# Reading the memory inside the first self-attention's loop, and one normalisation for two before the second cross-attention

## The chip, the cores and the metric

One Trainium2 chip, one core of it. A core has TensorE (PE, matrix products into PSUM), VectorE (DVE), ScalarE (ACT), GpSimd (POOL) and SyncE (SP, which starts the transfers), each with a queue of its own that it works off in order; they wait for one another by semaphores. The metric is the time of one execution on the device in microseconds, all in float32.

## The reference, cut to what matters

Two layers of a network run over 64 samples of 32 latent tokens with 128 features (2048 tokens), each with a context of 257 rows. Six blocks add to `x`, each after a normalisation:

```python
x = x + _L0_xattn_ref(_layernorm(x, axis=-1), ctx_1024, ctx_1024, ...)
x = x + _L0_attn_ref(_layernorm(x, axis=-1), L0_attn_Wq, ..., L0_attn_memory, L0_attn_memory_norm, L0_attn_memory_weight)
x = x + _L0_ffn_ref(_layernorm(x, axis=-1), ...)
x = x + _L1_xattn_ref(ctx_1024, _layernorm(x, axis=-1), ...)
x = x + _L1_attn_ref(...)
x = x + _L1_ffn_ref(...)
```

The first self-attention mixes ordinary attention with a memory that is read by the queries:

```python
a_dot = jnp.einsum('bnst,btnd->bsnd', probs, v4)
sigma_q = jax.nn.elu(q.reshape(B, S, N_QUERY, KV))
num = sigma_q @ memory
den = (sigma_q @ memory_norm)[..., None]
a_mem = (num / den).reshape(B, S, QH, D_HEAD)
w = jax.nn.sigmoid(memory_weight)
out = (a_dot * (1.0 - w) + a_mem * w).reshape(B, S, D_MODEL)
```

The second cross-attention gets `_layernorm(x)` and normalises it again, with a gain and an offset:

```python
ln = layer_norm(latents, g_latent, b_latent)   # (t - mu) * rsqrt(var + EPS) * gamma + beta
```

## The kernel before

The program is a chain of stages. Each stage is one or more blocks; a block gives every engine a piece of program, and at its end all engines meet before the next begins. Tensors stand with features on the 128 partitions and tokens along the free axis; `chunk(t, c)` is 512 of the 2048 tokens, so there are `NCH = 4` chunks. `core.bank` is PSUM, eight banks of 512 floats.

`layernorm` is a block of its own: for each chunk TensorE makes the mean (line 185), VectorE subtracts it (195), ScalarE squares (210), TensorE makes the variance (188), ScalarE takes logarithm and exponential for the reciprocal root (213, 215), and VectorE multiplies (199) and, if asked, applies gain and offset (202). Four chunks run staggered. It is called once before each block and twice before the second cross-attention, as `ln3` from `xT` to `yT` and as `ln4` from `yT` to `yT` with gain and offset.

`memory_attention_0` has three blocks. The first projects queries and keys into `qT` and `kT`. The second is the loop: 16 steps of four samples (128 tokens), two steps to one turn of a hardware loop (`Fori`), with n = 2 i + j the step. In a step GpSimd spreads keys and queries over the heads (650, 651), TensorE makes the scores of step n (675), VectorE takes the maximum and subtracts it (783, 785), ScalarE takes the exponential (740); VectorE sums, inverts and normalises the step before (792, 794, 796); TensorE transposes the probabilities of step n - 2 (666), ScalarE copies them as `pT` (727), TensorE multiplies them with the values (686), ScalarE masks the heads apart (735) and VectorE adds them up into `aT`, of step n - 3 (801); TensorE makes the values of step n (695) from tokens that ScalarE copied (754), and ScalarE copies the values (746). The order is written by hand: TensorE does transposes, scores, output product, values; ScalarE tokens, `pT`, exponential, mask, values; VectorE normalises, then maximum and subtraction, then the output. `S` uses banks 0 and 1, `TP`, `OP`, `VP` banks 2 to 4; banks 5 to 7 are unused in the loop.

The third block is the tail, which reads the memory for all 2048 tokens: VectorE takes the minimum with zero (837), ScalarE relu and exponential (859, 861), VectorE puts them together as the activated query `high` (841) and adds the attention's part to `xT` with its gate (843); TensorE makes the numerator (872) and the denominator for two groups of heads (874), ScalarE copies the numerator (864), VectorE inverts the denominators (845), TensorE turns them (877), ScalarE copies that (866), TensorE spreads them over the features (883), VectorE multiplies (850) and adds with the gate (854).

## Time and profile before

| | us |
|---|---|
| median of 3 runs | 1338.82 (1338.72 to 1343.13) |
| the profiled execution | 1347.86 |
| its span | 1346.1 |
| PE, DVE, ACT, POOL busy in it | 1183.1, 796.2, 731.1, 353.0 |

The profile is of one execution, whose span lies 1.8 us below its own time; a sum over its rows is made against 1347.86, and a difference is carried over to the median. Busy time counts what an engine works, waits are the gaps.
### The profile page before, as it was taken

The numbers are of one execution on the slowest core, as the hardware profiler recorded it, in microseconds if no ns is written. First come the engines' busy times: TensorE is split into PE (matmuls) and PEld (weight loads), VectorE is DVE, ScalarE is ACT, GpSimd is POOL, SyncE is SP. The second block draws the span as 40 slices with busy tenths as digits, with TensorE's granted clock in tenths as the row PEclk, the third lists the DMA queues.
The fourth block names the chain that finished last, engine by engine and source line by source line (L and its number), as shares of the span: only waits on it lengthen the run. The fifth ranks groups of instructions, "written<-read, shape, count | busy, mean of one in ns | idle before, by whom it ended". The sixth has DMA issues, their size and how long they took to land. (4 is left out here: it accounts for less than half of the span.)

```text
span 1346.1 us, 39879 instructions
## 1 busy us (share of the span) xinstructions
PE 1183.1 (88%) x14797; PEld 894.6 (66%) x14800; DVE 796.2 (59%) x2937; ACT 731.1 (54%) x1593; POOL 353.0 (26%) x734
## 2 busy tenths in 40 slices
PE   5899999966767699999987799999999999988865
PEld 2677777726655477777773688888888888732333
DVE  2677777756863356565655565555555555447267
ACT  2677777735862145444434455555555555354557
POOL 1121212126600011111110244334443344311132
PEclk8899999988986599999997899999999999998889
DMA  2433333100000333323220454445544455200001
GB/s 58 116 101 76 71 76 72 48 1 1 0 0 5 111 106 95 90 83 92 83 59 8 113 144 124 122 126 133 128 125 122 125 128 133 75 18 0 0 1 32
DMA packets 89480, 101.02 MB, mean 75 GB/s; under 512 B 13128, under 2 KB 78608, under 8 KB 89232
## 3 DMA queue, kind: packets, MB, share of 16 engines
q1 hardware_dynamic: 89360, 99.40, 28.3%
q8 instruction: 77, 1.26, 0.4%
q14 instruction: 43, 0.35, 0.1%
HBM read 87.62 MB, written 11.74 MB: 74 GB/s over the span
## 5 line engine op out<-in xcount | busy, mean ns | idle before, releaser
L1382 POOL TENSOR_TENSOR d_p<-d_p,d_rtotal 128x289 f32<-128x289 f32 x256 | 170.3, 665 | 246.5 <-DVE d_rtotal L1522 246.5
L1516 DVE CUSTOM_DVE_ANT_0 d_p<-bank,d_low 128x289 f32<-128x289 f32 x256 | 112.3, 439 | 180.6 <-PE bank L1411 180.6
L1481 ACT ACTIVATE d_p<-d_p,d_nmax 128x289 f32<-128x289 f32 x256 | 137.7, 538 | 98.7 <-DVE d_nmax L1516 98.6
L1424 PE MATMUL bank<-d_pT,d_xr 32*128 32x128 f32 x5120 | 160.9, 275 | 0.0
L1411 PE MATMUL bank<-x_keyT,d_q 128*128 128x289 f32 x512 | 154.8, 423 | 2.5 <-DVE d_nmax L1516 1.3
L1424 PEld LDWEIGHTS bank<-d_pT,d_xr 32*128 32x128 f32 x5120 | 148.7, 187 | 8.8 <-issue 1.5
L435 ACT ACTIVATE a_p<-a_p,a_nmax 128x257 f32<-128x257 f32 x256 | 109.4, 499 | 75.6 <-DVE a_nmax L468 75.6
L1146 PEld LDWEIGHTS bank<-c_w,c_hs 128*128 128x128 f32 x1024 | 120.9, 194 | 14.8 <-issue 14.8
L1530 DVE STREAM_TRANSPOSE d_pT<-d_p 128x320 f32<-128x320 f32 x256 | 128.4, 502 | 1.1 <-POOL d_p L1382 1.1
L1137 PE MATMUL bank<-yT,c_w 128*128 128x512 f32 x256 | 117.7, 604 | 4.7 <-DMA c_w<-in_L_ffn_w 4.7
L1146 PE MATMUL bank<-c_w,c_hs 128*128 128x128 f32 x1024 | 121.1, 277 | 0.0
L468 DVE CUSTOM_DVE_ANT_0 a_p<-bank,a_low 128x257 f32<-128x257 f32 x256 | 93.8, 423 | 41.8 <-PE bank L385 39.8
L1213 ACT ACTIVATE c_hs<-bank,c_w 128x512 f32<-128x512 f32 x128 | 87.5, 684 | 38.5 <-PE bank L1137 35.5
L1411 PEld LDWEIGHTS bank<-x_keyT,d_q 128*128 128x128 f32 x512 | 81.9, 189 | 33.3 <-DVE d_nmax L1516 18.0
L1205 ACT ACTIVATE x_keyT<-bank 128x512 f32<-128x512 f32 (+2 forms) x33 | 34.7, 1051 | 115.2 <-PE bank L1159 112.1
L1277 DVE SCALAR_TENSOR_TENSOR c_acc<-bank,c_gates,c_acc 128x128 f32<-128x128 f32 x128 | 36.0, 344 | 98.9 <-PE bank L1146 98.9
L1489 ACT ACTIVATE d_a<-bank 128x512 f32<-128x512 f32 x64 | 38.2, 597 | 85.2 <-PE bank L1424 85.2
L1137 PEld LDWEIGHTS bank<-yT,c_w 128*128 128x128 f32 x256 | 47.2, 194 | 52.9 <-issue 47.7
L1401 PEld LDWEIGHTS bank<-yT,x_wqk 128*128 128x128 f32 x512 | 67.7, 194 | 9.9 <-ACT d_q L1474 3.6
L1436 PEld LDWEIGHTS bank<-d_a,x_wvo 128*128 128x128 f32 x512 | 65.4, 191 | 13.1 <-issue 7.3
L1401 PE MATMUL bank<-yT,x_wqk 128*128 128x128 f32 x512 | 68.7, 278 | 2.4 <-ACT d_q L1474 2.4
L1436 PE MATMUL bank<-d_a,x_wvo 128*128 128x128 f32 x512 | 68.2, 277 | 2.0 <-ACT d_a L1489 0.7
(289 smaller groups left out, 2094.4 us busy)
## 6 DMA issues: line engine op xcount, KB each, us to landing
d_xr<-key_rows SPq DMA_DIRECT2D x256, 160.0 KB, 3.1
d_low<-mask_low SPq DMA_DIRECT2D x64, 144.5 KB, 3.4
a_ctT<-in_ctxT SPq DMA_DIRECT2D x64, 128.5 KB, 2.1
a_low<-mask_low SPq DMA_DIRECT2D x64, 128.5 KB, 3.0
c_ct<-in_ctx SPq DMA_DIRECT2D x64, 128.0 KB, 2.3
key_rows<-c_ct SPq DMA_DIRECT2D x128, 64.0 KB, 2.0
c_w<-in_L_ffn_w SPq DMA_DIRECT2D x8, 514.0 KB, 3.8
xT<-in_xT SPq DMA_DIRECT2D x4, 256.0 KB, 3.6
```

The lines of the kernel that those rows point to most:

```text
L435: nc.scalar.activation(P[:, r % 2, g, :], P[:, r % 2, g, :], ACT.Exp, bias=nmax[:, r % 2, g:g + 1], scale=-1.0).then_inc(exp_made, 1)
L468: nc.vector.tensor_tensor_reduce(P[:, r % 2, g, :], S[g], low[:, r % RING, :], -1.0, 3.4e38, ALU.add, ALU.min, accum_out=nmax[:, r % 2, g: ...
L1137: nc.tensor.matmul(UP[k], w[:, j, 128 * k:128 * k + 128], chunk(core.yT, c), start=True, stop=True).then_inc(up_made, 1)
L1146: ins = nc.tensor.matmul(Y[s % 2][:, m, :], hs[:, s % 2, k, 128 * m:128 * m + 128], w[:, j, HID + 128 * k:HID + 128 * k + 128], start=(k = ...
L1382: nc.gpsimd.tensor_tensor(p, p, rtotal[:, b % 2, g:g + 1].broadcast_to([128, KEYS]), ALU.mult).then_inc(normed, 1)
L1401: ins = nc.tensor.matmul(Q[:, 128 * h:128 * h + 128], wqk[:, 4 * r + h, :], latT[:, bass.ds((i * 2 + ahead) * 128, 128)], start=True, stop ...
L1411: nc.tensor.matmul(S[u % 2], q[:, b // 4, b % 4, 4 * g:4 * g + 4, :].rearrange("p h q -> p (h q)"), keyT[:, bass.ds(i * EIGHT + b, 1), :]. ...
L1424: ins = nc.tensor.matmul(O[j], xr[rows, b % 2, k, :], pT[rows, b % 2, :, 32 * k:32 * k + 32], start=(k == 0), stop=(k == BLOCKS - 1))
L1436: ins = nc.tensor.matmul(OUT, wvo[:, h, :], a[:, ago % 2, h].rearrange("p b q -> p (b q)"), start=(h == 0), stop=(h == HEADS - 1))
L1481: nc.scalar.activation(p, p, ACT.Exp, bias=nmax[:, b % 2, g:g + 1], scale=-1.0, accum_out=total[:, b % 2, g:g + 1]).then_inc(exp_made, 1)
L1516: nc.vector.tensor_tensor_reduce(P[:, b % 2, g, 0:KEYS], S[u % 2], low[:, b % 4, :], -1.0, 3.4e38, ALU.add, ALU.min, accum_out=nmax[:, b % ...
L1530: nc.vector.transpose(pT[:, b % 2, g, :], P[:, b % 2, g, :]).then_inc(turned, 1)
```

## The change

The third block of `memory_attention_0` is gone. Its work is done by a function `retrieve(n)` in the queue of each of the three engines, once in every step of the loop, behind the step's own work. `due(n, delay)` tells whether a part is due: a chunk c has its parts in the steps 3 c + delay. Minimum, relu and exponential have delay 0, putting together 1, numerator and denominator 2, the inverse, its turning and the copy of the numerator 3, the copy of the turned inverse 4, the spreading 5, product and gated addition 6. The attention's own gated addition of a chunk (`attended`) follows when its four steps of output are done, in the steps 7, 11 and 15, and once behind the loop. The parts use banks 5 to 7, one chunk at a time, so further waits guard each bank and the small tiles. The loops are no longer hardware loops but written out, on all four engines.

The two normalisations before the second cross-attention become one from `xT` to `yT` with gain and offset; the variance goes into the logarithm as var (1 + EPS) + EPS squared, which is what the two roots come to one behind the other. A constant tile for it is set at the start of the program.

```diff
--- before.py
+++ after.py
...
-def layernorm(core, name, src, dst, gamma=None, beta=None):
+def layernorm(core, name, src, dst, gamma=None, beta=None, twice=False):
...
-                    nc.scalar.activation(chunk(rstd, s - 1), var[:, s - 1, :], ACT.Ln, bias=core.eps[:, 0:1]).then_inc(log_ready, 1)
+                    nc.scalar.activation(chunk(rstd, s - 1), var[:, s - 1, :], ACT.Ln, bias=(core.eps_twice if twice else core.eps)[:, 0:1],
+                                         scale=1.0 + EPS if twice else 1.0).then_inc(log_ready, 1)
...
+            NUM, SPREAD = core.bank[:, 5, :], core.bank[:, 7, :]
+            DEN, TURNED = core.bank[:, 6, 0:8], core.bank[0:8, 6, 128:256]
...
+            STEP = 3
             block = loop.enter_context(nc.Block())
+
+            def due(n, delay):
+
+                c, rest = divmod(n - delay, STEP)
+                return c if rest == 0 and 0 <= c < NCH else None
...
-                peeled(pool, GROUPS // 2, body)
+                unrolled(GROUPS // 2, body)
...
+                    retrieve(n)
+
+                def retrieve(n):
+
+                    c = due(n, 2)
+                    if c is not None:
+                        pe.wait_ge(elu_made, c + 1)
+                        if c:
+                            pe.wait_ge(num_kept, c)
+                            pe.wait_ge(turned_kept, c)
+                        nc.tensor.matmul(NUM, mem[:], chunk(high, c), start=True, stop=True)
+                        for m in range(4):
+                            ins = nc.tensor.matmul(DEN[:, 2 * m:2 * m + 2], high[:, 512 * c + 128 * m:512 * c + 128 * m + 128], norm[:], start=True, stop=True)
+                        ins.then_inc(num_made, 1)
+                    c = due(n, 3)
+                    if c is not None:
+                        pe.wait_ge(inverted, c + 1)
+                        nc.tensor.transpose(TURNED, inverse[:], core.ident[:]).then_inc(turned, 1)
+                    c = due(n, 5)
+                    if c is not None:
+                        pe.wait_ge(turned_kept, c + 1)
+                        if c:
+                            pe.wait_ge(weighed, c)
+                        for m in range(4):
+                            ins = nc.tensor.matmul(SPREAD[:, 128 * m:128 * m + 128], place[0:8, m].rearrange("r s d -> r (s d)"), inverse_t[:], start=True, stop=True)
+                        ins.then_inc(spread, 1)
...
-                with pe.Fori(2, GROUPS // 2) as i:
+                for i in range(2, GROUPS // 2):
...
+                def retrieve(n):
+
+                    c = due(n, 0)
+                    if c is not None:
+                        nc.scalar.activation(chunk(high, c), chunk(qT, c), ACT.Relu).then_inc(relu_made, 1)
+                        act.wait_ge(clipped, c + 1)
+                        nc.scalar.activation(chunk(low, c), chunk(low, c), ACT.Exp).then_inc(expd, 1)
+                    c = due(n, 3)
+                    if c is not None:
+                        act.wait_ge(num_made, c + 1)
+                        act.wait_ge(elu_made, c + 1)
+                        nc.scalar.activation(chunk(low, c), NUM, ACT.Copy).then_inc(num_kept, 1)
+                    c = due(n, 4)
+                    if c is not None:
+                        act.wait_ge(turned, c + 1)
+                        if c:
+                            act.wait_ge(spread, c)
+                        nc.scalar.activation(inverse_t[:], TURNED, ACT.Copy).then_inc(turned_kept, 1)
...
                     values(0, j)
+                    retrieve(j)
...
+                def retrieve(n):
+
+                    c = due(n, 0)
+                    if c is not None:
+                        nc.vector.tensor_scalar(chunk(low, c), chunk(qT, c), 0.0, None, ALU.min).then_inc(clipped, 1)
+                    c = due(n, 1)
+                    if c is not None:
+                        dve.wait_ge(relu_made, c + 1)
+                        dve.wait_ge(expd, c + 1)
+                        nc.vector.scalar_tensor_tensor(chunk(high, c), chunk(low, c), -1.0, chunk(high, c), ALU.add, ALU.add).then_inc(elu_made, 1)
+                    c = due(n, 3)
+                    if c is not None:
+                        dve.wait_ge(num_made, c + 1)
+                        if c:
+                            dve.wait_ge(turned, c)
+                        nc.vector.reciprocal(inverse[:], DEN).then_inc(inverted, 1)
+                    c = due(n, 6)
+                    if c is not None:
+                        dve.wait_ge(num_kept, c + 1)
+                        dve.wait_ge(spread, c + 1)
+                        nc.vector.tensor_tensor(chunk(low, c), chunk(low, c), SPREAD, ALU.mult).then_inc(weighed, 1)
+                        dve.wait_ge(weighed, c + 1)
+                        nc.vector.scalar_tensor_tensor(chunk(core.xT, c), chunk(low, c), gate[:, 2:3], chunk(core.xT, c), ALU.mult, ALU.add).then_inc(chain, 1)
+
+                def attended(c):
+
+                    dve.wait_ge(o_copied, 4 * c + 4)
+                    dve.wait_ge(chain, c + 1)
+                    nc.vector.scalar_tensor_tensor(chunk(core.xT, c), chunk(aT, c), gate[:, 3:4], chunk(core.xT, c), ALU.mult, ALU.add)
...
+                        retrieve(i * 2 + j)
+                        if (i * 2 + j) % 4 == 3 and i * 2 + j >= 7:
+                            attended((i * 2 + j - 7) // 4)
...
+                attended(NCH - 1)
...
-    layernorm(core, "ln3", core.xT, core.yT)
...
-        layernorm(core, "ln4", core.yT, core.yT, affine[:, 2:3], affine[:, 3:4])
+        layernorm(core, "ln3", core.xT, core.yT, affine[:, 2:3], affine[:, 3:4], twice=True)
```

TensorE in the loop, before: one step from the values of a step on (695 values, 666 transposes, 675 scores, 686 output product), inside the hardware loop.

```order
L695 MATMUL bank<-wb_wv,b_yg 128x128 x4
L666 MATMUL bank<-ident,b_p 128x128 x4
L671 REGISTER_ALU
L675 MATMUL bank<-b_kb,b_qb 128x128 x4
L686 MATMUL bank<-b_pT,b_vb 128x128 x4
L695 MATMUL bank<-wb_wv,b_yg 128x128 x4
```

And after, from the values of step 5 to those of step 6 (709 values, 721 numerator, 723 denominator, 735 spreading, 680 transposes, 689 scores, 700 output product).

```order
L709 MATMUL bank<-wb_wv,b_yg 128x128 x4
L721 MATMUL bank<-b_high,wb_mem 128x512
L723 MATMUL bank<-b_norm,b_high 128x2 x4
L735 MATMUL bank<-b_inverse_t,b_place 128x128 x4
L680 MATMUL bank<-ident,b_p 128x128 x4
L689 MATMUL bank<-b_kb,b_qb 128x128 x4
L700 MATMUL bank<-b_pT,b_vb 128x128 x4
L709 MATMUL bank<-wb_wv,b_yg 128x128 x4
```

Numerator, denominator and spreading now stand between a step's values and the transposes and scores of the next.

ScalarE in the loop, before (746 values, 754 tokens, 727 `pT`, 740 exponential, 735 mask), from the values of step 2 on, the same order as in the hardware loop:

```order
L746 ACTIVATE b_vb<-bank 32x4x32 x4
L754 ACTIVATE b_yg<-yT 128x512
L727 ACTIVATE b_pT<-bank 128x512
L740 ACTIVATE b_p<-b_p 128x512
L735 ACTIVATE b_odiag<-bank,b_own_head 128x4x32 x4
L746 ACTIVATE b_vb<-bank 32x4x32 x4
```

And after, from the values of step 3 on (786 values, 800 relu, 802 exponential, 807 numerator, 794 tokens, 767 `pT`, 780 exponential of step 4).

```order
L786 ACTIVATE b_vb<-bank 32x4x32 x4
L800 ACTIVATE b_high<-b_qT 128x512
L802 ACTIVATE b_low<-b_low 128x512
L807 ACTIVATE b_low<-bank 128x512
L794 ACTIVATE b_yg<-yT 128x512
L767 ACTIVATE b_pT<-bank 128x512
L780 ACTIVATE b_p<-b_p 128x512
```

Three operations now stand between the values and the tokens of the next step, in every third step.

VectorE after, in step 6 (863 output, 870 minimum, 881 inverse, 886 product, 888 gated addition, 854 to 858 the normalising of that step):

```order
L863 TENSOR_REDUCE b_aT<-b_odiag 128x128
L870 TENSOR_SCALAR b_low<-b_qT 128x512
L881 RECIPROCAL b_inverse<-bank 128x8
L886 TENSOR_TENSOR b_low<-b_low,bank 128x512
L888 SCALAR_TENSOR_TENSOR xT<-b_low,wb_gate,xT 128x512
L854 TENSOR_REDUCE b_total<-b_p 128x16
L856 RECIPROCAL b_rtotal<-b_total 128x16
L858 TENSOR_TENSOR b_p<-b_p,b_rtotal 128x512
```

Before, the output was followed straight by the sum of line 792; four operations now stand between.

## Rows read from the trace of the kernel before

**Rows 1.** Stage table: start:end, length; busy (instructions) per engine; PEclk granted clock; DMA share; GB/s.
```profile
302.00:323.00 21.00, 11.91 (x68) 11.26 (x69) 12.07 (x15) 8.16 (x22) 14.99 (x41) 0.76 0.00 1
323.00:380.00 57.00, 41.24 (x342) 38.77 (x341) 47.00 (x73) 47.67 (x135) 31.91 (x88) 1.00 0.00 0
391.50:418.00 26.50, 21.40 (x73) 16.62 (x74) 12.87 (x21) 6.91 (x14) 0.00 (x0) 0.50 0.00 1
```

**Rows 2.** Timeline, one loop step: start, length, engine, line, operation, [idle before <-releaser].
```profile
361.05 0.63 ACT L754 ACTIVATE b_yg<-yT 128x512 f32 x1
...
361.70 0.60 ACT L727 ACTIVATE b_pT<-bank 128x512 f32<-128x512 f32 x1
361.79 0.69 DVE L785 TENSOR_TENSOR b_p<-bank,b_top 128x512 f32<-128x512 f32 x1
...
362.35 1.16 PE L686 MATMUL bank<-b_pT,b_vb 128*128 128x128 f32 x8 [1.32 <-ACT b_pT L727]
...
362.52 0.63 ACT L740 ACTIVATE b_p<-b_p 128x512 f32<-128x512 f32 x1 [0.22 <-DVE b_p L785]
...
363.35 1.06 PE L695 MATMUL bank<-wb_wv,b_yg 128*128 128x128 f32 x8
...
363.63 1.14 ACT L735 ACTIVATE b_odiag<-bank,b_own_head 128x128 f32<-128x128 f32 x4 [0.48 <-PE bank L686]
...
364.24 0.60 PE L666 MATMUL bank<-ident,b_p 128*128 128x128 f32 x4
...
364.64 1.09 ACT L746 ACTIVATE b_vb<-bank 32x128 f32<-32x128 f32 x4
364.68 1.06 PE L675 MATMUL bank<-b_kb,b_qb 128*128 128x128 f32 x8
365.75 0.63 ACT L754 ACTIVATE b_yg<-yT 128x512 f32 x1
365.77 0.69 DVE L783 TENSOR_REDUCE b_top<-bank 128x16 f32<-128x512 f32 x1 [0.69 <-PE bank L675]
```

**Rows 3.** Timeline: first and last operation of the tail, and the next normalisation.
```profile
391.80 0.63 ACT L859 ACTIVATE b_high<-b_qT 128x512 f32<-128x512 f32 x1 [1.37 <-PEq L623]
...
416.95 0.75 DVE L854 SCALAR_TENSOR_TENSOR xT<-b_qT,wb_gate,xT 128x512 f32<-128x512 f32 x1
417.97 1.28 ACT L206 ACT_TABLE_LOAD   x1 [9.09 <-PEq L823]
```

**Rows 4.** Timeline: TensorE in the tail.
```profile
400.76 2.06 PE L872 MATMUL bank<-b_high,wb_mem 128*128 128x512 f32 x2
...
402.61 1.71 PE L874 MATMUL bank<-b_norm,b_high 128*128 128x2 f32 x8
...
408.93 7.19 PE L883 MATMUL bank<-b_inverse_t,b_place 32*128 32x128 f32 x32 [0.35 <-ACT b_inverse_t L866]
```

**Rows 5.** Timeline, start of the loop; last, line 796 (times ns: min/median/max).
```profile
310.37 3.82 DVE L796 TENSOR_TENSOR b_p<-b_p,b_rtotal 128x512 f32<-128x512 f32 x1
...
313.25 0.40 POOL L651 TENSOR_TENSOR b_qb<-b_qT,b_own_head 128x128 f32<-128x128 f32 x1
...
317.22 0.77 DVE L796 TENSOR_TENSOR b_p<-b_p,b_rtotal 128x512 f32<-128x512 f32 x1
...
317.91 0.68 DVE L783 TENSOR_REDUCE b_top<-bank 128x16 f32<-128x512 f32 x1
...
323.70 0.69 DVE L783 TENSOR_REDUCE b_top<-bank 128x16 f32<-128x512 f32 x1 [1.99 <-PE bank L675]
...
L796 DVE TENSOR_TENSOR b_p<-b_p,b_rtotal x16: 691/692/3821, 310.4 to 383.2; 128x512 f32<-128x512 f32 x16
```

**Rows 6.** Timeline: first operations of the two normalisations and of the stage behind.
```profile
718.99 1.28 ACT L206 ACT_TABLE_LOAD   x1 [7.54 <-PEq L1043]
...
732.38 1.28 ACT L206 ACT_TABLE_LOAD   x1 [1.01 <-PEq L165]
...
746.49 3.27 PEld L1454 LDWEIGHTS bank<-ident,yT 128*128 128x128 f32 x16 [3.79 <-issue]
```

More of the change, by code:

```diff
@@ L35, in __init__ @@
         self.rows_moved = self.sem("rows_moved")
-        self.eps = self.sb("eps", [128, 1])
+        self.eps, self.eps_twice = self.sb("eps", [128, 1]), self.sb("eps_twice", [128, 1])
         self.spent, self.spent_sems = ExitStack(), []
@@ L155, in _ @@
             nc.gpsimd.memset(core.eps[:], EPS).then_inc(built, 1)
+            nc.gpsimd.memset(core.eps_twice[:], EPS * EPS).then_inc(built, 1)
             pool.wait_ge(built, 1)
@@ L637, in memory_attention_0 @@
             t_made, t_copied, o_made, o_masked, o_copied = (sem(f"b_{n}") for n in ("t_made", "t_copied", "o_made", "o_masked", "o_copied"))
+            low, high = sb("b_low", [128, TOK]), sb("b_high", [128, TOK])
+            inverse, inverse_t = sb("b_inverse", [128, 8]), sb("b_inverse_t", [8, 128])
+            NUM, SPREAD = core.bank[:, 5, :], core.bank[:, 7, :]
+            DEN, TURNED = core.bank[:, 6, 0:8], core.bank[0:8, 6, 128:256]
+            clipped, relu_made, expd, elu_made, num_made, num_kept, inverted, turned, turned_kept, spread, weighed, chain = (
+                sem(f"b_{n}") for n in ("clipped", "relu_made", "expd", "elu_made", "num_made", "num_kept", "inverted", "turned", "turned_kept", "spread", "weighed", "chain"))
+            STEP = 3
             block = loop.enter_context(nc.Block())
+            def due(n, delay):
+                c, rest = divmod(n - delay, STEP)
+                return c if rest == 0 and 0 <= c < NCH else None
             @block.gpsimd
@@ L766, in _ @@
                     values(1, j)
-                with act.Fori(2, GROUPS // 2) as i:
+                    retrieve(2 + j)
+                for i in range(2, GROUPS // 2):
                     for j in range(2):
@@ L810, in body @@
                             output(i, j - 3)
+                        retrieve(i * 2 + j)
+                        if (i * 2 + j) % 4 == 3 and i * 2 + j >= 7:
+                            attended((i * 2 + j - 7) // 4)
                 body(0, 0)
                 body(1, 1)
-                with dve.Fori(2, GROUPS // 2) as i:
+                for i in range(2, GROUPS // 2):
                     body(i, 2)
```

58 lines of the change are left out of this document (removed).

## The prediction

> **What bounds the kernel now.** I read the stage table first, then one step of the self-attention loop in the timeline, then the tail behind the loop, then the three normalisations. The whole program is a chain of stages, each ended by a block boundary that all engines pass, so the last engine of each stage counts, and shares of the whole span say little. The change touches two stretches: the first self-attention (loop and tail), and the two normalisations before the second cross-attention.
>
> The loop does 16 steps of 128 tokens. In its steady part, 323 to 380 us [rows 1], no engine is full (VectorE 47.0, ScalarE 47.7, TensorE 41.2 of 57 us), so a ring of waits bounds it. One step [rows 2] shows it: ScalarE copies pT (361.70); 0.65 later TensorE starts the output product (362.35); 1.28 later ScalarE masks it (363.63); 1.01 later it copies the values (364.64), 1.11 later the tokens (365.75), and as after the copy of tokens at 361.05, 0.65 later the next pT. Sum 0.65 + 1.28 + 1.01 + 1.11 + 0.65 = 4.70, just the distance of the two token copies (365.75 - 361.05). ScalarE rests only 0.70 in it (0.22 ahead of the exponential, 0.48 ahead of the mask), VectorE 0.69 (ahead of the maximum), TensorE 1.32 (ahead of the output product); the brackets behind the rows say so. Those three gaps are all the cover there is.
>
> The tail reads the memory: 391.80 to the start of the next normalisation at 417.97 [rows 3], 26.2 us. TensorE works in it at a granted clock of 0.50, 1.2 of 2.4 GHz [rows 1], and its products are most of it: four times 2.06 for the numerator plus 1.71 for the denominator, then 7.19 to spread [rows 4].
>
> **The change part by part.** *The tail goes*: -26.2 us. What comes back is the four gated additions of the attention; three lie in the loop, the last stays behind it with its 0.75 (the same form as the multiply-add at 416.95) [rows 3]. Before, the boundary behind the last addition took 0.27 (417.97 - 416.95 - 0.75) and there was one from loop to tail of the same kind; one of the two goes with the tail.
>
> *The same work in the loop.* Per chunk of 512 tokens, every third step, prices at the full clock, which the loop has [rows 1]: TensorE gets numerator, denominator and spread. Their rows, halved, allow up to 2.06 / 2 = 1.03, 1.71 / 2 = 0.86 and 7.19 / 4 / 2 = 0.90; each holds the drain of its last product, which the next one covers, so I take 0.86 for each. ScalarE gets relu and exponential (0.63 each [rows 3]) and the copy of the numerator (0.60, as pT [rows 2]), less the overlap of neighbours, 0.63 against 0.55 from row to row, so 1.63; and a copy of 8x128, about one of the four in row 364.64, 0.2 to 0.3. VectorE gets five operations, none longer than the 0.75 of row 416.95 and the reciprocal of eight columns far shorter, and on average one gated addition of 0.75: 3 to 3.5 in all.
>
> Where they stand decides, and there are three kinds of step (n is the step, remainder by three):
> 1. Remainder 1: the small copy goes into ScalarE's ring, 4.70 + 0.2 = 4.9. VectorE's subtraction of one (0.7) takes its gap of 0.69.
> 2. Remainder 2: numerator, denominator and (from n = 5) spread stand behind the value product, and in front of the transposes that the next pT needs. From pT: 0.65 to the output product, 1.00 to the values (362.35 to 363.35) [rows 2], 0.89 for these (363.35 to 364.24 is their pitch, by eight instructions of 0.11), then 3 x 0.86, and transposes and semaphore 0.65. Sum 5.77, so +1.1.
> 3. Remainder 0: TensorE is now late, so the ring starts at its transposes: 0.44 to the scores, 1.09 to the maximum (364.24, 364.68, 365.77) [rows 2], 0.72 to the subtraction (361.79, a step earlier), 0.73 to the exponential (362.52), 0.55 to the mask, 1.01 and 1.11 as before, then relu, exponential and numerator copy 1.63, and tokens 0.65. That is 7.93; less the 0.65 from transposes to pT, 7.28, so +2.6.
>
> Three steps cost 17.9 where they cost 14.1. The ends differ: n = 2 has no spread (+0.2), n = 3 starts nearly on time (+2.4), n = 12 has only the numerator copy (+1.5), n = 14 only a spread, which fits into 1.32. Sum for n = 2 to 14: 0.2 + 2.4 + 0.2 + 1.1 + 2.6 + 0.2 + 1.1 + 2.6 + 0.2 + 1.1 + 1.5 + 0.2 + 0 = 13.4.
>
> The added wait with something behind it: in kind 3 TensorE waits for VectorE's reciprocal to turn it, and the transposes and scores of the next step queue behind. But VectorE reads those scores only after its product, multiply-add and normalising, which follow the reciprocal by 0.7 + 0.75 + 1.7, more than the 0.44 + 1.09 that TensorE needs. I take 0; the other end is the 1.5 of that pair, four times.
>
> *The start.* In the first step VectorE's normalising product took 3.82 instead of a median of 0.69, while GpSimd ran one operation after the other up to 313.65 [rows 5]. Now the minimum stands ahead of it in that burst. I let it take over the wait; then total, reciprocal and product follow behind the burst instead of inside it, so the next maximum starts about 1.5 later. If the minimum is not held up, the product is, as now, and ScalarE's two new operations cost 1.04. I take 1.5.
>
> *VectorE beside GpSimd.* At 310.37 VectorE's product of two SBUF tiles lost 3.1 us; at 317.22 the same product met GpSimd's stream and lost 0.08 [rows 5]. The new operations that read SBUF alone stand mostly right behind the output reduction, near the end of GpSimd's burst. Each may cost 0 to 3.1; I take the near end, since of the 16 normalising products, one in each step, these two alone took over 0.70; with something for bad luck 0.5 on the sum. The Trainium skill, page "SBUF — State Buffer", section "Who interferes with whom", says that an operation with two SBUF inputs fully blocks against a GpSimd operation that reads SBUF, and that issue order decides. By that rule the first row is the normal case, the second is luck; with one more wait like the first the 0.5 would be 3.1. How far it can go is the last rival.
>
> *The clock.* TensorE rests longer in kind 3. Before, its clock was 0.76 in the start-up, where it had such rests, and the step from 317.91 to 323.70 took 5.79 instead of 4.70 [rows 1, 5]. So a fall costs about 1.1 each; none to four of them, I take two, +2.2.
>
> *Loops written out.* The closing branch has no part in the ring, whose five parts fill the 4.70, so writing the loop out is worth 0. More instructions cost 0: the tail is written out too, and its 32 products follow one another at their pitch [rows 4].
>
> Loop and tail together: -26.2 - 0.3 + 13.4 + 1.5 + 0.75 + 0.5 + 2.2 = -8.1.
>
> *Normalisations.* The first starts at 718.99, the second at 732.38, the next stage at 746.49 [rows 6]. The merged one does what the second did, with gain and offset, on another source, and other numbers in the logarithm's operands: it takes 746.49 - 732.38 = 14.1, and 732.38 - 718.99 = 13.4 go. Nothing ran under the first alone; all engines wait at its end. What follows is tied to its end, not to a transfer.
>
> Sum: -8.1 - 13.4 = -21.5. On the profiled execution: 1347.9 - 21.5 = 1326.4. The median of the runs stands 9 us below that execution; the difference carries over: 1338.8 - 21.5 = 1317.3, say 1317.5.
>
> **The rivals.**
> A, *the work fits better* (16%): TensorE's additions find more room than I give, and only ScalarE's 4 x (1.63 + 0.25) = 7.5, with the start and the end, come back. Then -26.5 + 7.5 + 1.5 + 0.75 = -16.8, in all 1308.6. For it: no engine would be full at 16.0 per three steps. Against: the order in the queue puts the three products in front of transposes.
>
> B, *the clock falls in the loop* (16%) at every kind-3 step and stays down for a step more: eight slow steps instead of two, +6.6, 1324.
>
> C, *nothing is hidden* (13%): the three additions per chunk stand in series in the ring, 2.6 + 1.9 + 3.5 = 8.0, times four 32, less the 6 or so that go into gaps: the loop grows by the 26 that the tail gives, and only the normalisation is gained, 1325.4. For it: kind 3 puts ScalarE's part straight behind TensorE's. Against: VectorE's part is off the ring in every kind. This is also the case in which the change does not do what it says.
>
> D, *slower* (3%): GpSimd holds VectorE back. Each of the 14 bursts behind the first two steps hits a VectorE operation at its start and keeps it the 3.1 of row 310.37: +43, so 1361. From 7 such meetings on the gain is gone, from 9 it is slower by over 0.5%. Against it: row 317.22, and the median of the sixteen. The skill's rule, if it held for every new operation, would lead this way.
>
> **How the numbers follow.** The forecast, 1311 to 1323, has 52%. Low end 1308 (A mostly in), high end 1328 (B and C in): about 15% is left out. 0.5% of 1338.8, about what a measurement here can tell from none, is 6.7: all of the forecast, A, B, and most of C are faster by more. Faster 0.92, same 0.05, slower 0.03.
>
> **What would show it.** In the profile after: no stretch of 26 us behind the loop; distances of the maximum's starts in threes of about 4.9, 5.8, 7.3; TensorE waiting in kind 3 and full in kind 2; the last addition, then at about 407 us the normalisation (410 with the falls); one normalisation of 14.1. Wrong would be: threes of 16 (A), a granted clock below 0.9 in the loop (B), VectorE operations of over 1.5 us in the loop beyond the first (D).

## The result and the profile after

| | us |
|---|---|
| kernel before, median of 4 runs | 1338.77 (1335.35 to 1343.13) |
| kernel after, median of 4 runs | 1320.51 (1318.64 to 1327.99) |
| ratio, with its 95% interval | 0.9851 [0.9823, 0.9879] |
| profiled execution: before, after | 1347.86, 1318.64 |
| its span: before, after | 1346.1, 1316.9 |

The change saves 18 us by the medians, 20 by the ratio, whose interval is 16 to 24. The forecast was 1317.5 in a range of 1308 to 1328: the time fell inside, 3 us above it. The two profiled executions differ by 29.2 us: that of before stands 9.1 above its median, that of after 1.9 below.

The stage table after, over the start of the self-attention, its steady part and its end; the columns are those of [rows 1].
```profile
302.00:323.00 21.00, 15.71 (x93) 14.35 (x94) 12.93 (x19) 10.25 (x26) 15.25 (x39) 0.76 0.00 0
323.00:380.00 57.00, 42.72 (x326) 38.98 (x325) 45.16 (x74) 41.49 (x118) 30.92 (x78) 0.97 0.01 1
380.00:405.00 25.00, 15.54 (x111) 13.60 (x109) 19.28 (x29) 16.01 (x48) 3.35 (x8) 0.86 0.00 1
```
Against [rows 1] TensorE alone got a little fuller in the steady part (41.24 to 42.72 of 57 us, a part of that at the lower clock), though TensorE, ScalarE and VectorE all have more to do per step: the steps became longer. ScalarE went from 47.67 to 41.49, VectorE from 47.00 to 45.16. What bounds the loop is still a ring of waits, and now a different one in each kind of step. The third row stands where before 26.5 us at a clock of 0.50 stood; it is the end of the loop itself, at a mean clock of 0.86.

Two steps of the timeline after, remainder 2 and then 0. They answer to [rows 2], and the three TensorE rows from 354.25 to 355.99 to [rows 4].
```profile
351.73 0.57 ACT L767 ACTIVATE b_pT<-bank 128x512 f32<-128x512 f32 x1
352.36 1.16 PE L700 MATMUL bank<-b_pT,b_vb 128*128 128x128 f32 x8 [1.26 <-ACT b_pT L767]
353.35 1.06 PE L709 MATMUL bank<-wb_wv,b_yg 128*128 128x128 f32 x8
...
354.25 1.02 PE L721 MATMUL bank<-b_high,wb_mem 128*128 128x512 f32 x2
...
355.11 0.95 PE L723 MATMUL bank<-b_norm,b_high 128*128 128x2 f32 x8
...
355.99 1.15 PE L735 MATMUL bank<-b_inverse_t,b_place 8*128 8x128 f32 x8
...
357.07 0.66 PE L680 MATMUL bank<-ident,b_p 128*128 128x128 f32 x4
357.56 1.06 PE L689 MATMUL bank<-b_kb,b_qb 128*128 128x128 f32 x8
357.76 0.60 ACT L767 ACTIVATE b_pT<-bank 128x512 f32<-128x512 f32 x1 [1.00 <-PE bank L680]
...
358.66 0.69 DVE L845 TENSOR_REDUCE b_top<-bank 128x16 f32<-128x512 f32 x1 [2.61 <-PE bank L689]
359.38 0.69 DVE L847 TENSOR_TENSOR b_p<-bank,b_top 128x512 f32<-128x512 f32 x1
...
360.11 0.63 ACT L780 ACTIVATE b_p<-b_p 128x512 f32<-128x512 f32 x1 [1.74 <-DVE b_p L847]
360.64 1.12 ACT L775 ACTIVATE b_odiag<-bank,b_own_head 128x128 f32<-128x128 f32 x4
...
361.64 1.09 ACT L786 ACTIVATE b_vb<-bank 32x128 f32<-32x128 f32 x4
361.70 0.27 PE L728 MATMUL bank<-ident,b_inverse 128*8 128x128 f32 x1 [1.24 <-DVE b_inverse L881]
...
362.75 0.63 ACT L800 ACTIVATE b_high<-b_qT 128x512 f32<-128x512 f32 x1
...
363.29 0.61 ACT L802 ACTIVATE b_low<-b_low 128x512 f32<-128x512 f32 x1
...
363.93 0.60 ACT L807 ACTIVATE b_low<-bank 128x512 f32<-128x512 f32 x1
364.42 0.62 ACT L794 ACTIVATE b_yg<-yT 128x512 f32<-128x512 f32 x1
...
364.94 0.59 ACT L767 ACTIVATE b_pT<-bank 128x512 f32<-128x512 f32 x1
```
Read it from one copy of pT to the next. From 351.73 to 357.76, 6.03 us, TensorE has no gap after 352.36: output, values, numerator, denominator, spread, transposes, and ScalarE waits 1.00 for the last of them. From 357.76 to 364.94, 7.18 us, the ring runs as forecast: the transposes came late, so scores, maximum (VectorE waited 2.61 for it), subtraction and exponential (ScalarE waited 1.74) are late, and from 360.11 on ScalarE has no gap: mask, values, relu, exponential, numerator, tokens, pT. The step ahead took 4.65.

The start of the loop, for [rows 5] (VectorE, L870 is the minimum that the change put there, L858 the normalising product), then the end of the attention for [rows 3], then the merged normalisation and the stage behind it for [rows 6].
```profile
305.35 0.69 DVE L845 TENSOR_REDUCE b_top<-bank 128x16 f32<-128x512 f32 x1 [6.24 <-PE bank L689]
...
306.68 2.50 DVE L870 TENSOR_SCALAR b_low<-b_qT 128x512 f32<-128x512 f32 x1
...
310.09 0.69 DVE L858 TENSOR_TENSOR b_p<-b_p,b_rtotal 128x512 f32<-128x512 f32 x1
310.70 0.68 DVE L845 TENSOR_REDUCE b_top<-bank 128x16 f32<-128x512 f32 x1
```
```profile
404.33 0.75 DVE L894 SCALAR_TENSOR_TENSOR xT<-b_aT,wb_gate,xT 128x512 f32<-128x512 f32 x1
405.35 1.28 ACT L207 ACT_TABLE_LOAD   x1 [2.12 <-PEq L625]
```
```profile
707.96 1.28 ACT L207 ACT_TABLE_LOAD   x1 [9.15 <-PEq L1073]
...
720.74 1.94 POOL L1413 COPY x_keyT<-yT 128x2048 f32<-128x2048 f32 x1 [30.43 <-POOLq L166]
```
The gated addition at 404.33 is the last work of the attention, and the normalisation follows at 405.35, against 417.97. The merged normalisation takes 720.74 - 707.96 = 12.78.

**By stages.** Differences of starts, from the profiled executions; the loop is counted from its first to its last maximum.

| | to the first maximum | loop | last maximum to normalisation | two stages between | normalisation(s) | cross-attention | the rest |
|---|---|---|---|---|---|---|---|
| before | 307.25 | 72.63 | 38.09 | 301.02 | 27.51 | 428.00 | 171.60 |
| after | 305.35 | 86.71 | 13.29 | 302.61 | 12.78 | 426.51 | 169.65 |
| difference | -1.9 | +14.1 | -24.8 | +1.6 | -14.7 | -1.5 | -1.9 |

The changed stretches give -10.7 and -14.7, the unchanged ones -3.8, in all -29.2. The -3.8 is not shown to come from the change: over all profiles below, with and without it, the first maximum starts between 302.3 and 307.9, and the rest behind the cross-attention takes 168.7 to 173.6.

### The profile page after: what moved, and what is told of

Read it like the earlier page. It is cut to its first block and busy times, and to the rows that moved or that the text cites. A ratio compares the mean times of both kernels' runs of the same rounds, so it can differ in the third digit from the quotient of the medians.

```text
span 1316.9 us, 39669 instructions
## 1 busy us (share of the span) xinstructions
PE 1160.9 (88%) x14784; PEld 884.8 (67%) x14787; DVE 788.2 (60%) x2932; ACT 720.6 (55%) x1583; POOL 358.0 (27%) x735
## 5 line engine op out<-in xcount | busy, mean ns | idle before, releaser
L1167 PEld LDWEIGHTS bank<-yT,c_w 128*128 128x128 f32 x256 | 47.1, 194 | 52.8 <-issue 47.2
```

Of the source, the lines that this page charges most:

```text
L1167: nc.tensor.matmul(UP[k], w[:, j, 128 * k:128 * k + 128], chunk(core.yT, c), start=True, stop=True).then_inc(up_made, 1)
```

## The experiments

Each row of "pT" below is the distance of one copy of pT to the next in the middle of the loop, in the order remainder 1, 2, 0, at full clock. It cuts the ring at its own place; the starts of the maximum shift a part of the same three steps to a neighbour (5.97, 5.29, 6.61 for the same 17.87). The last column is one execution each and carries the differences of stretches that no edit touches; the 1336.45 and the 1302.48, for instance, are the lowest of their 12 and 6 runs. So a row is read by its distances, and by medians where the text gives them.

| kernel | pT distances | three steps | first to last maximum | profiled execution |
|---|---|---|---|---|
| before | 4.70 4.70 4.71 | 14.1 | 72.63 | 1347.86 |
| loops written out alone | 4.63 4.63 4.64 | 13.9 | 67.85 | 1336.45 |
| after | 4.65 6.03 7.18 | 17.9 | 86.71 | 1318.64 |
| numerator doubled | (falls of clock) 6.88 7.19 | | 93.19 | 1329.63 |
| relu doubled | 4.65 6.03 7.70 | 18.4 | 89.52 | 1322.16 |
| weighing doubled | 4.97 6.03 7.18 | 18.2 | 87.78 | 1318.94 |
| products in the gap | 4.66 6.59 6.16 | 17.4 | 81.43 | 1319.45 |
| and the spread one step later | 4.65 5.41 6.16 | 16.2 | 79.17 | 1310.97 |
| everything spaced | 4.63 5.14 5.73 | 15.5 | 75.80 | 1302.48 |

### The kernel after, once more

No edit.

> The changed kernel once more, beside the parts of it. The sum of my prediction gives -21.5 us on the median; the first comparison gave -18.3, and the two profiled executions lie 29 apart. If the profiled execution of before was only a long one of its kind, the medians again differ by 18 to 22 and the loop and tail of this kernel's profile are again about 11 us shorter than before's.

Median 1320.89 of 6 runs (1315.69 to 1327.60) against 1339.62 of 23 of the kernel before: 0.9844 [0.9811, 0.9877]. The profile repeats the first almost to the digit: loop 86.80, last maximum to normalisation 13.29, normalisation 12.78. The result stands, and differences of a tenth of a microsecond between steps at full clock can be read.

### One part alone: the loop

```diff
+    layernorm(core, "ln3", core.xT, core.yT)
...
-        layernorm(core, "ln3", core.xT, core.yT, affine[:, 2:3], affine[:, 3:4], twice=True)
+        layernorm(core, "ln4", core.yT, core.yT, affine[:, 2:3], affine[:, 3:4])
```
(against the kernel after)

> Memory reading in the loop, but the two normalisations kept. My sum: loop and tail give -8.1, so about 1331; the profile after shows -10.7 from the loop's first maximum to the next normalisation, so rather 1328. Rival C (nothing hidden) would give 1338 to 1341, rival A 1322.

Median 1336.29 of 12 runs, 0.9959 [0.9940, 0.9978], so -5.5 us (-8.0 to -2.9). In the profile, first maximum to normalisation is 101.3, -9.4. Here too the medians show less than the profiles. Both of the expectation's figures (-8.1 and about -10.7) lie outside the interval of the medians, the first by a tenth. The minimum at the start took another course:
```profile
309.03 5.38 DVE L870 TENSOR_SCALAR b_low<-b_qT 128x512 f32<-128x512 f32 x1
```
GpSimd's last operation of that stretch began at 313.70, and the minimum ended 0.7 later: it waited out the whole stream. In the kernel after it took 2.50 over the same code. At full clock the loop otherwise had the steps of the table, 4.66, 6.03, 7.18; two of its steps of remainder 1 met a fall of the clock and took 6.08 and 5.40.

### One part alone: the normalisation

```diff
+def layernorm(core, name, src, dst, gamma=None, beta=None, twice=False):
...
-    layernorm(core, "ln3", core.xT, core.yT)
...
-        layernorm(core, "ln4", core.yT, core.yT, affine[:, 2:3], affine[:, 3:4])
+        layernorm(core, "ln3", core.xT, core.yT, affine[:, 2:3], affine[:, 3:4], twice=True)
```
(against the kernel before)

> The merged normalisation alone, self-attention as before. My sum: -13.4, so about 1325.5. If the stage behind also gains from a higher clock at its start, as the profile after shows (14.7 instead of 13.4), up to 2 more. If the difference of the medians was small because the merging gives less than its span, it would show here as less than 11.

Median 1331.67 of 6 runs, 0.9922 [0.9895, 0.9950], so -10.4 us (-14.1 to -6.7). That is less than the 11 which the expectation had set as the sign that merging gives less than its span, though the interval holds both. In its profile the merged one took 12.79. Two rows of the stage table, the pair of the kernel before and of the kernel with the loops written out (the next experiment), show what the pair cost:
```profile
718.90:746.40 27.50, 20.81 (x32) 7.42 (x32) 12.95 (x20) 17.45 (x26) 0.00 (x0) 0.75 0.00 0
```
```profile
709.60:733.70 24.10, 16.76 (x32) 5.89 (x33) 13.04 (x20) 17.28 (x26) 0.00 (x0) 0.93 0.00 0
```
The same instructions took 27.5 us at a mean granted clock of 0.75 and 24.1 at 0.93. Removing one is worth 27.5 - 12.8 = 14.7 against the first row and 24.1 - 12.8 = 11.3 against the second; the median lies nearer to the second. The clock in this stretch differs from profile to profile. The four with the pair took 27.5, 27.4, 26.3 and 24.1 (mean clock 0.75, 0.75, 0.82, 0.93). The nine with the merged one took 12.8 to 13.0, and 13.98 in one, at 0.74 in place of 0.87. The unprofiled executions don't show what they had there.

### One part alone: loops written out

```diff
-                peeled(pool, GROUPS // 2, body)
+                unrolled(GROUPS // 2, body)
...
-                with pe.Fori(2, GROUPS // 2) as i:
+                for i in range(2, GROUPS // 2):
```
(against the kernel before; the same for ScalarE and VectorE)

> Before, with only the four loops of the self-attention written out. I priced this at 0: within 1 us of before, and the same 4.70 us per step in the profile. If closing branches or register operations cost something in the ring, steps fall below 4.70 and up to 3 us go; if fetching more instructions costs, it is slower.

Median 1341.11 of 12 runs, 0.9999 [0.9979, 1.0019]. The steps took 4.63 in place of 4.70, 0.9 us over the loop, too little for the medians. The 0.07 lies between the output product and ScalarE's mask, 1.20 (353.73 to 354.93) in place of the 1.28 in the prediction; the other waits of the ring agree within 0.01. The bigger difference of this profile is at the start, where the first two normalising products met the same burst of GpSimd:
```profile
306.32 1.00 DVE L796 TENSOR_TENSOR b_p<-b_p,b_rtotal 128x512 f32<-128x512 f32 x1
...
310.36 0.99 DVE L796 TENSOR_TENSOR b_p<-b_p,b_rtotal 128x512 f32<-128x512 f32 x1
```
1.00 and 0.99, where the kernel before has 3.82 and 0.77 [rows 5]. So the wait of a product in that burst is not a property of the two operations: it depends on how they meet.

### The kernel before, once more

No edit; one more profiled execution.

> The kernel before once more, for a second profiled execution. Its first one took 1347.9, 9 above its median, and against it the kernel after saved 29 us stage by stage, while the medians differ by 18. Theory: 7 to 11 us of the 29 are unchanged work that ran at a lower granted clock in that one execution. Then this profile is shorter than 1347.9 by 5 to 12 us, with first maximum to the normalisation behind the loop at 108 to 110.7 and the two later normalisations at 24 to 27.5 in place of 27.5. Rival: the kernel before always has those stretches and the median of its runs is short for another reason; then they come back within 0.3. The first normalising product beside GpSimd: 3.8 again if the order of issue alone settles it, anything from 0.7 to 3.8 if small shifts do.

1347.46, and 1339.38 for another execution on the same chip. Stage by stage it is the first profile again: first maximum to normalisation 110.80, the pair 27.40, cross-attention 428.01, the product 3.84. The rival held, not the theory: both profiled executions of the kernel before have these lengths, and the 39 others, in four groups, have medians of 1338.8 to 1340.0 (1333.57 to 1347.83). Six of the 39 took over 1345, so an execution as long as the profiled ones also comes without a profile; what makes it long stays open.

### Which engine sets each kind of step: one operation doubled

Against the kernel after, each with the result of the first copy unused.
```diff
                         nc.tensor.matmul(NUM, mem[:], chunk(high, c), start=True, stop=True)
+                        nc.tensor.matmul(NUM, mem[:], chunk(high, c), start=True, stop=True)
```

> The changed kernel with the numerator's product made twice, one behind the other (0.86 us more on TensorE in the steps of kind 2, four of them). By my ring TensorE is on the path in those steps: the first has slack, the others pay in full, 2.6 to 3.4 us in all. If TensorE's work hides in its waits, nothing.

The steps of remainder 2 grew from 6.03 to 6.88, by 0.85 each: one product more, at its whole pitch. TensorE is what these steps wait for, and a product costs there the 0.86 of the forecast. The first of the four, which the expectation took as covered, was paid as well (7.40 in place of 6.54). The steps of remainder 0 stayed at 7.19. The four extra products are 3.4; the loop grew by 6.5 against the first profile of the kernel after. The rest is the clock, in the stage table over the steady part:
```profile
323.00:380.00 57.00, 43.72 (x296) 39.34 (x295) 41.70 (x67) 38.79 (x109) 28.50 (x72) 0.91 0.00 1
```
0.91 in place of 0.97. The steps of remainder 1 took 6.19, 6.02 and 5.67 at the three falls, against 5.57 (one fall), 4.65 and 4.66: 0.6 + 1.4 + 1.0 = 3.0.

```diff
+                        nc.scalar.activation(scratch[:, 0:512], chunk(qT, c), ACT.Relu)
                         nc.scalar.activation(chunk(high, c), chunk(qT, c), ACT.Relu).then_inc(relu_made, 1)
```

> The kernel after with ScalarE's relu of a chunk done twice (the first one into a spare tile), four more operations of 0.63, 0.55 from row to row. Theory: in the steps of remainder 0 (n = 3, 6, 9) ScalarE's part of the retrieval is in the ring, so each of these grows by 0.55, from 7.28 to 7.85; n = 0 has the relu beside VectorE's minimum, which takes 2.5, and grows by 0. First maximum to last 1.65 longer, steps of remainder 1 and 2 unchanged at 4.9 to 6.0 and 5.3. Rival: in remainder 0 VectorE or TensorE is last and ScalarE has room; then 0. Should the granted clock fall once more or once less, 0.9 either way.

Remainder 0 went from 7.18 to 7.70, 0.52 each; remainder 1 and 2 stayed at 4.65 and 6.03. ScalarE's part is in the ring of remainder 0 alone.
```profile
342.05 1.09 ACT L787 ACTIVATE b_vb<-bank 32x128 f32<-32x128 f32 x4
343.17 0.63 ACT L801 ACTIVATE b_scratch<-b_qT 128x512 f32<-128x512 f32 x1
343.70 0.61 ACT L802 ACTIVATE b_high<-b_qT 128x512 f32<-128x512 f32 x1
344.22 0.61 ACT L804 ACTIVATE b_low<-b_low 128x512 f32<-128x512 f32 x1
344.86 0.60 ACT L809 ACTIVATE b_low<-bank 128x512 f32<-128x512 f32 x1
```
From the first of the two relus to the second is 0.53. The loop grew by 2.8 (2.7 against the second profile), of which 3 x 0.52 = 1.6 is this; the clock fell at two steps of remainder 1, which took 6.06 and 5.43 in place of 5.57 and 4.65, and that is the other 1.3.

```diff
+                        nc.vector.tensor_tensor(scratch[:, 0:512], chunk(low, c), SPREAD, ALU.mult)
                         nc.vector.tensor_tensor(chunk(low, c), chunk(low, c), SPREAD, ALU.mult).then_inc(weighed, 1)
```

> The kernel after with VectorE's weighing of a chunk (product of the kept numerator and the spread reciprocals) done twice, the first one into a spare tile: four more operations of about 0.7 in the steps of remainder 2 (n = 5, 8, 11, 14). Theory: there TensorE sets the pace and VectorE has 0.69 of gap beside it, so the four cost 0 to 0.3 each, 0 to 1.2 in all. Rival: VectorE is what the steps wait for (no engine is full, but its part is the largest addition, 3 to 3.5 per chunk); then 0.7 each, 2.8 in all. Should the granted clock fall once more or once less, 0.9 either way.

The expectation put the operation into remainder 2 by mistake. With delay 6 it stands in VectorE's queue in the steps 6, 9, 12 and 15, of remainder 0, and what it delays is the next step. ScalarE there, in step 7:
```profile
348.40 0.63 ACT L781 ACTIVATE b_p<-b_p 128x512 f32<-128x512 f32 x1 [1.02 <-DVE b_p L848]
348.94 1.12 ACT L776 ACTIVATE b_odiag<-bank,b_own_head 128x128 f32<-128x128 f32 x4
```
Remainder 1 went from 4.65 to 4.97, the other two stayed at 6.03 and 7.18. VectorE's subtraction, and with it the exponential, are now so late that the mask starts straight behind the exponential, 2.15 after pT in place of 1.83. So VectorE is in no ring of the kernel after, but in remainder 1 its cover is only 0.3 to 0.4: of 0.6 to 0.7 more, 0.3 comes through in the middle of the loop. The four operations cost 0.30, 0.31, 0.47 and 0.61, in all 1.7, where the expectation gave 0 to 1.2 and its rival 2.8. From the first maximum to the normalisation the kernel grew by 1.6.

### The retrieval's products in TensorE's gap

In the kernel before TensorE rests 1.32 us ahead of the output product in each step, in the kernel after 2.27 and 1.26 in remainder 1 and 2. Against the kernel after, numerator, denominator and spread go there (the small turning stays behind the values); then, in a second kernel, against the first, the spread one step later still.
```diff
                         scores(i, j, first)
+                        retrieve(i * 2 + j)
                         if not first:
                             output(i, j - 2)
```
```diff
-            STEP, SPREAD_AT, TURN_AT = 3, 5, 3
+            STEP, SPREAD_AT, TURN_AT = 3, 6, 3
```

> TensorE's numerator, denominator and spread stand between a step's scores and its output product, where it waits 1.32 us in a plain step, instead of behind the values; all delays as in the changed kernel. If my kinds of step are right, the transposes and scores are no longer pushed back by 2.6: a group of three falls from 17.9 to about 17.1 (kind 3 from 7.3 towards 6.5), loop and tail shorter by about 3 us. If the order in TensorE's queue does not matter (ScalarE's or VectorE's share alone lengthens the loop), it stays at 17.9.

> As gap, and the spread one step later (delay 6), so that no step has all three products. By my ring the step with numerator and denominator alone overruns the 1.32 by 0.4 instead of 1.3: groups of three of about 16.0 to 16.3, loop and tail about 6.5 us shorter than in the changed kernel. By a bound from full engines (16.0 by ScalarE's additions) it would stop near 16.0 too; a rival in which VectorE bounds stays near 17.

The place alone took the three steps from 17.9 to 17.4 only: three products in a row, 2.6 us, don't fit into a rest of 1.3. Remainder 0 gained 1.0, since the transposes are no longer late, and remainder 2 lost 0.56, since the output product is. TensorE in that step of the first kernel:
```profile
350.11 1.10 PE L721 MATMUL bank<-b_high,wb_mem 128*128 128x512 f32 x2 [0.35 <-ACT b_inverse_t L818]
351.05 0.95 PE L723 MATMUL bank<-b_norm,b_high 128*128 128x2 f32 x8
351.92 1.15 PE L731 MATMUL bank<-b_inverse_t,b_place 8*128 8x128 f32 x8
353.01 1.16 PE L700 MATMUL bank<-b_pT,b_vb 128*128 128x128 f32 x8
```
pT was copied at 350.39 and ready by 351.0; the output product came 2.0 later. With the spread in another step remainder 2 is 5.41, and three steps 16.2: a further -1.2. The profiled executions were 1319.45 and 1310.97, and neither kernel has others. First maximum to normalisation is 93.9 and 91.7 against 100.0: 6.1 and 8.3 shorter, where 3 and 6.5 were expected. That 1319.45 is no shorter than the 1318.64 of the kernel after comes from stretches that the edit doesn't touch, which took 6.9 more in that execution. Part of the 6.1 stands at the start, where the step of n = 2 took 4.79 in place of 6.54.

### Everything spaced

Beside that, one chunk's numerator, its copy and the small operations move to other steps, so that each kind of step holds at most one pair of ScalarE's additions and one or two of TensorE's: relu and exponential with the spread in remainder 0, numerator and denominator in 1, both copies and the turning in 2.
```diff
-            STEP, SPREAD_AT, TURN_AT = 3, 5, 3
+            STEP, SPREAD_AT, TURN_AT = 3, 6, 5
...
-                    c = due(n, 2)
+                    c = due(n, 4)
                     if c is not None:
                         pe.wait_ge(elu_made, c + 1)
...
-                    c = due(n, 3)
+                    c = due(n, 5)
                     if c is not None:
                         act.wait_ge(num_made, c + 1)
```
(against the first kernel with the products in the gap; and ScalarE's small copy 4 to 5, VectorE's subtraction of one 1 to 2, its reciprocal 3 to 4)

> As gap_spread6, and the parts spread over remainders: minimum, relu, exponential with delay 0, putting together 2, numerator, denominator and inverse 4, turning and both copies on ScalarE 5, spread, product and gated addition 6. No step has more than 1.1 us of additions on ScalarE. By the ring: groups of three of about 15.9, the loop about 8 us shorter than in the changed kernel, so about 1312 against 1320 in the medians. If the time is not in the placing but in the work, it stays at 1320.

Median 1308.74 of 6 runs (1302.48 to 1316.67), 0.9772 [0.9736, 0.9809] to the kernel before: -30.5 us, and the interval lies just below that of the kernel after, [0.9811, 0.9877]. The steady part of its stage table:
```profile
323.00:380.00 57.00, 47.02 (x376) 43.32 (x377) 52.82 (x84) 47.79 (x135) 31.03 (x76) 1.00 0.00 1
```
Three steps take 15.5, and TensorE's clock doesn't fall in the steady part. VectorE is at 52.8 of 57: it is near to being the bound, which it was not with the work bunched.

## Why the prediction was right

**The three kinds of step: right.** Forecast 4.9, 5.77 and 7.28, together 17.9; measured, from pT to pT, 4.65, 6.03 and 7.18, together 17.9. The doubled product showed TensorE as the bound of remainder 2 and its pitch as 0.85; the doubled relu showed ScalarE in the ring of remainder 0, 0.52 each. Two terms were a quarter of a microsecond off and cancel: the small copy costs nothing in remainder 1 (4.65, against 4.63 in the loop written out), and remainder 2 has 0.26 more, since the spread holds TensorE for 1.08 (355.99 to 357.07) and not for 0.86.

**The added wait at zero: right.** TensorE waited 1.24 for the reciprocal (361.70), and the scores behind it were done at 363.3, before VectorE came to them at 364.6.

**The start: mis-sized.** Forecast +1.5 to the next maximum; it came 1.5 earlier (5.35 against 6.86), since the minimum was held for 2.50 where the product had been held for 3.82. The third step, with a fall of the clock and the first chunk's products, gave that back (7.38 against 5.79), so from the first to the fourth maximum the sum is +0.2, where 1.7 was forecast with n = 2. With the wait of 5.38, as in the loop alone, the first step took 8.24, 1.4 more than before, and the forecast's size comes back. That the burst holds VectorE's first such operation was right; how long was not foreseeable from one row.

**The clock: one fall in place of two.** In the steady part the clock fell once (the step of remainder 1 that took 5.57), and the price was 5.57 - 4.65 = 0.9, where 1.1 was forecast: +0.9 in place of +2.2. How often it falls differs between executions: one fall in the steady part in both profiles of the kernel after, two in that of the loop alone, over the same code. A second fall lies behind the last step and stretched the last output products (2.08 in place of 1.16), so that part from the last maximum gave -24.8, where the terms for tail, boundary and last addition add up to -25.7.

**VectorE beside GpSimd: little.** Behind the start the new minimum took 0.56 to 0.58 and the product 0.81 at most: no single operation inside the steps over 1.1, so rival D has no row for it. The Trainium skill, page "SBUF — State Buffer", section "Who interferes with whom", says that of two contenders the second to issue fully blocks until the first is through. The rows agree where VectorE gets in behind one operation of GpSimd, as the product of 0.81 did. They add that against an unbroken stream it got in after six operations (2.50), or only at the stream's end: the 5.38 of the loop alone, and also the 3.82 before, which ended 0.54 behind GpSimd's last operation (313.25 to 313.65).

**Loop and tail: -8.1 forecast, -10.7 in the profiles, -5.5 (-8.0 to -2.9) in the medians of the loop alone.** The 2.6 to the profile are the start (1.5) and the clock (1.3), less 0.9 behind the loop, and the 0.5 for bad luck that wasn't needed; 0.2 is left over. In the medians the term came out 2.6 too large, and no run shows why. **Normalisation: -13.4 forecast, -14.7 in the profiles, -10.4 (-14.1 to -6.7) in the medians.** The merged pass was forecast at 14.1, the price of the second pass at a clock of 0.74; it took 12.8 at 0.87, and 13.98 in the one profile where it met 0.74. Against the pair at a clock of 0.93 the term is 11.3. I made the sum against one profiled execution and carried the difference over to the median as it was. That step was too generous: the profiles differ by 29.2, the medians by 18.3. Taken one by one, both terms came out about 3 larger than in the medians, while a start priced too dear and a clock priced too slow went the other way. So the mechanism of the loop is shown step by step, but that the total came within 3 us is partly luck.

**What stays open.** The loop alone is worth 9.4 in the profiles and 5.5 in the medians, and the pair's clock doesn't touch it. One candidate is the start: with the product at 1.00 in the kernel with the loops written out, first maximum to normalisation took 105.8 in place of 110.7, and were most executions of the kernel before like that, the loop's gain would be 5 or so. But the product took 3.82, 3.84 and 3.85 in the three profiles of kernels with the old loop, and that kernel, whose profile was 11 us shorter, has the median of the kernel before. The other executions give only time and mean clock (0.951 at 1333.57, 0.945 at 1339.38, against 0.942 at 1347.46), so this was not settled. The two parts alone add up to -15.9 in medians and together give -18 to -21, within the intervals.

**The rivals.** A (three steps at 16) is out for this kernel by the 17.9, C (the loop grows by 26) by the 14.1. B is out with a clock of 0.97. In D, nine waits of 3.1 less the 21.5 are 6.4, just under the 6.7 of 0.5%, so ten would be needed. The spaced kernel shows that A was not wrong about the room, only about this order: at 15.5 there was still more of it.

## What to carry to other kernels

Where a loop is bound by a ring of waits and no engine is full, price added work step by step: find for each place in the queue which ring passes there, and count only what stands in it. Work that moves into such a loop should be dealt out in pieces smaller than the rest it is to fill, one engine's piece per step; the tail of 26 us cost 4.0 us per chunk in one order and 1.6 in another (17.9 and 15.5 for three steps, against 13.9), and first to last maximum grew by 14 and by 3, of which the start and the falls of the clock are a part. And when a removed stretch ran at a low clock in the profile, quote its worth as a range down to what the same instructions took at a higher clock, and take the difference of medians, not of two profiled executions, as the result.

## What the runs showed of the chip

The same minimum of VectorE met the same stream of GpSimd and took 2.50 or 5.38, where it takes 0.42 in the tail of the kernel before; the product took 3.82 to 3.85 or 1.00, where it mostly takes 0.69. Later on they took 0.54 to 0.58 and 0.69 to 0.92. GpSimd's operation that lost to them took 0.58 to 0.94 in place of 0.40. Which of these comes out repeats from one profile of a kernel to the next (2.50 and 2.52, 3.82 and 3.84), and changes with edits a microsecond away.

Writing the loop out took 0.07 from each of its steps (4.70 to 4.63), though the branch stands in none of the waits that I had counted as the ring; the rows place the 0.07 ahead of the mask, and what shortens that wait was not tested. In this ring of waits a fall of TensorE to 0.50 made a step of remainder 1 longer by 0.7 to 1.5 (4.65 to between 5.40 and 6.19).
